# Halves side by side in the linear attention of a graph layer, with a new order of steps

## The reference

```python
x2 = _layer_norm(x, ln1_g, ln1_b)
q = (x2 @ wq + bq).reshape(B, L, N_HEAD, D_HEAD)
k = (x2 @ wk + bk).reshape(B, L, N_HEAD, D_HEAD)
v = (x2 @ wv + bv).reshape(B, L, N_HEAD, D_HEAD)
qp = _fourier_kernel(q, proj_mat)     # p = q @ proj_mat / 8, then cos(p), sin(p)
kp = _fourier_kernel(k, proj_mat)
kv = jnp.einsum('blhm,blhd->bhmd', kp, v)
attn = jnp.einsum('blhm,bhmd->blhd', qp, kv)
attn = attn.reshape(B, L, D_MODEL) @ wo + bo
```

## Time and profile before

| | before |
|---|---|
| median of 3 runs | 1335.42 us (1334.34 to 1340.76) |
| profiled execution, its time | 1334.61 us |
| its span | 1332.8 us |
| mean granted TensorE clock | 0.971 |
| PE busy | 94% of the span |
| DVE, ACT, POOL busy | 57%, 47%, 26% |

### The profile page before, as it was taken

The page is one execution under the profiler, slowest core; times in us unless marked ns, Lnnn a source line. Parts: engine busy times, 40 slices in busy tenths (PEclk is TensorE's granted clock), DMA queues, the critical chain, the costliest instruction groups (busy, mean ns, idle before and its releaser), DMA issues. The chain is left out here.

```text
span 1332.8 us, 19542 instructions
## 1 busy us (share of the span) xinstructions
PE 1247.7 (94%) x7017; PEld 1088.1 (82%) x7017; DVE 766.2 (57%) x1212; ACT 631.6 (47%) x917; POOL 340.5 (26%) x296
## 2 busy tenths in 40 slices
PE   6989889999999999999957999799999999899997
PEld 4556689999999999999946787699997887788874
DVE  7979625455655556565553376577774321556546
ACT  8175534555555555555554533332233442455544
POOL 1400003241423232332220201056662433021000
PEclk9999999999999999999976999899999799999999
DMA  8011310111020202020214645432335232620112
GB/s 207 10 29 25 78 36 1 33 35 54 12 66 0 66 0 66 0 66 0 67 45 150 216 151 172 137 107 81 92 91 192 74 93 62 211 72 14 50 32 93
DMA packets 72193, 99.41 MB, mean 75 GB/s; under 512 B 27241, under 2 KB 52165, under 8 KB 71631
## 3 DMA queue, kind: packets, MB, share of 16 engines
q1 hardware_dynamic: 68684, 86.11, 22.5%
q0 software_dynamic: 3456, 12.58, 3.1%
HBM read 77.04 MB, written 21.63 MB: 74 GB/s over the span
## 5 line engine op out<-in xcount | busy, mean ns | idle before, releaser
L1140 POOL TENSOR_TENSOR cos_sin_lo<-cos_sin,cos_sin_hi 125x1024 fp32r<-125x1024 f32 (+1 forms) x40 | 95.8, 2396 | 351.2 <-ACT cos_sin_hi L1214 351.2
L1201 ACT ACTIVATE cos_sin<-part_turn 125x512 f32<-125x512 f32 (+1 forms) x80 | 50.1, 627 | 152.7 <-DVE part_turn L1329 152.7
L468 PE MATMUL p_cnt<-hot_s,hot_d 125*125 125x418 bf16 x540 | 113.8, 361 | 1.8 <-DVE hot_d L401 1.8
L705 PE MATMUL p_h<-x 128*125 128x512 f32 x400 | 109.3, 400 | 0.0
L399 DVE TENSOR_SCALAR hot_s<-iota_h,ends 125x1250 bf16<-125x1250 f16 x180 | 98.2, 546 | 14.6 <-PE p_cnt L468 12.5
L468 PEld LDWEIGHTS p_cnt<-hot_s,hot_d 125*125 125x125 bf16 x540 | 63.3, 140 | 51.6 <-DVE hot_d L401 40.6
L1414 PE MATMUL p_w<-x,mix_hi_v 128*128 128x416 f32 (+1 forms) x384 | 105.2, 355 | 0.0
L1414 PE MATMUL p_w<-x,mix_hi_k 128*128 128x416 f32 (+1 forms) x384 | 104.2, 352 | 0.0
L1414 PE MATMUL p_w<-x,mix_hi_q 128*128 128x416 f32 (+1 forms) x384 | 104.1, 352 | 0.0
L966 PE MATMUL rows_in_psum<-h_hi,a_lo 125*125 125x342 f32 x300 | 96.8, 323 | 3.0 <-DVE a_lo L910 3.0
L1327 DVE TENSOR_SCALAR whole_turns<-p_p 125x512 f32<-125x512 f32 (+1 forms) x80 | 54.4, 680 | 77.0 <-PE p_p L1465 74.4
(11 more groups left out here) (302 smaller groups left out, 3169.8 us busy)
## 6 DMA issues: line engine op xcount, KB each, us to landing
x_in<-in_x_dram SPq DMA_DIRECT2D x30, 448.0 KB
attn_dram<-attn_t SPq DMA_DIRECT2D x8, 625.0 KB, 3.9
at_in<-attn_dram SPq DMA_DIRECT2D x10, 500.0 KB, 4.6
x_rows<-in_x_dram SPq DMA_DIRECT2D x10, 448.0 KB
x_in<-gnn_dram SPq DMA_DIRECT2D x10, 448.0 KB
out_dram<-rows SPq DMA_DIRECT2D x10, 448.0 KB
mix_in_v<-in_L_mix_wv_dram SPq DMA_DIRECT2D x8, 512.0 KB, 6.0
mix_in_k<-in_L_mix_wk_dram SPq DMA_DIRECT2D x8, 512.0 KB, 4.7
```

Of the source, the lines that this page charges most:

```text
L468: last = pe.matmul(p_cnt[0:T, t % 2, n, 0:w], hot_d[:, j, 0:T], hot_s[:, j, a:a + w], start=False, stop=False)
L705: last = pe.matmul(p_h[0:T, i % 2, n, :], left[i % 2][:, k, :], right[:, k, cols], start=(k == 0 and m == 0), stop=(k == K8 - 1 and m == 2))
L1140: pool.tensor_tensor(full(cs_lo, k), full(cs, k), f32(full(cs_hi, k)), ALU.subtract).then_inc(s_cslo[0], 1)
L1201: act.activation(step_view(cs, k, 1), rows(part, k), ACT.Sin, scale=TWO_PI)
```

## The change

Three products lose one of their three matmul terms. A high part and a low part now lie side by side in one operand, and the half of the array that held the other head or zeros holds the second part.

- `v_both` has, for each head, 64 columns of high part and 64 of low part. `accumulate_kv` multiplies them by the low and the high features of that head alone, 256 columns, into one of two banks of `p_kv_at`. The two halves of its output are added up later, in SBUF: ACT copies one half (`kv_sum`), DVE adds the other (`add_kv`), and both split the sum into `kv_both`.
- `kv_both` has high and low part side by side. `attend` takes the features' low and high part, 8 matmuls a step. The output of each head has two halves, in the two partition halves. ACT's `keep_attention` copies one, 64 partitions, for each head, and the new `add_attention` on DVE adds the other. `s_atk`, for which the next `attend` waits, is now given by DVE. `p_at` is the second bank of `p_kv_at`, so `accumulate_kv(j, 0)` waits for it too.
- `q_both` has a head's high part in one partition half and its low part in the other; `proj_both` has the projection in both. `query_phases` has 4 matmuls. ACT and DVE write the queries in halves of 64 partitions.
- All four compute engines get a new order in `pair`. `cos_sin` is cut in two, `sines` and `keep_hi`. `key_phases` of step k+2 stands at the start of round k, no longer at its end. On DVE `phases` comes one place sooner, and the splits of the graph weight (`low_of_w`, `high_of_w`) are spread over the last pass.

Each product now also holds the term lo*lo.

```diff
-        q_hi = sb("q_hi", [128, N], F32R)
-        q_lo = sb("q_lo", [128, N], F32R)
+
+        q_both = sb("q_both", [128, 2, N], F32R)
+        proj_both = sb("proj_both", [128, 2, KMAP], F32R)
         v_t = sb("v_t", [128, N])
-        v_hi = sb("v_hi", [T, NT, 128], F32R)
-        v_lo = sb("v_lo", [T, NT, 128], F32R)
+
+        v_both = sb("v_both", [T, NT, 2, 2, DH], F32R)
...
+        kv_sum = sb("kv_sum", [128, 4, DH])
+
+        kv_both = sb("kv_both", [128, 4, 2, DH], F32R)
...
-        p_kv = ps("p_kv", [128, 512])
-        p_at = ps("p_at", [128, 512])
+        p_kv = ps("p_kv_at", [128, 2, 512])
+        p_at = p_kv[:, 1]
```

ACT and GpSimd:

```diff
+            pool.wait_ge(s_prep, 3)
+            for n, half in enumerate((proj_lo, proj_hi)):
+                pool.tensor_tensor(proj_both[:, n], f32(half[:, 0]), f32(half[:, 1]), ALU.add).then_inc(s_prep, 1)
...
-                keep_lo(j, 0)
...
+                if more:
+                    keep_lo(j + 1, 0)
...
+            keep_lo(0, 0)
...
                 act.wait_ge(s_tr, 4 * j + 4)
+                act.activation(kv_sum[:], p_tr[:, :, DH:2 * DH], ACT.Copy, scale=1.0 / KMAP).then_inc(s_kvs, 1)
+                act.wait_ge(s_kvs, 2 * j + 2)
                 for h in range(2):
-                    last = act.activation(kv_hi[:, 2 * h:2 * h + 2, h * DH:(h + 1) * DH],
-                                          p_tr[:, 2 * h:2 * h + 2, h * DH:(h + 1) * DH], ACT.Copy, scale=1.0 / KMAP)
+                    last = act.activation(kv_both[:, 2 * h:2 * h + 2, h], kv_sum[:, 2 * h:2 * h + 2], ACT.Copy)
                 last.then_inc(s_trhi, 1)
...
-            def cos_sin(j, k):
+            def sines(j, k):
...
+
+            def keep_hi(j, k):
                 act.wait_ge(s_cs, done(j, k))
...
-                act.activation(attn_t[:, c * CHUNK:(c + 1) * CHUNK], p_at[:, 0:CHUNK], ACT.Copy).then_inc(s_atk, 1)
+                for h in range(2):
+                    head = slice(h * DH, (h + 1) * DH)
+                    last = act.activation(attn_t[head, c * CHUNK:(c + 1) * CHUNK], p_at[head, h * CHUNK:(h + 1) * CHUNK], ACT.Copy)
+                last.then_inc(s_atc, 1)
```

The queue of ACT at the end of a pass:

```diff
                 keep_attention(j, 2)
-                cos_sin(j, 9)
                 if more:
+                    sines(j + 1, 0)
                     keep_v(j + 1, 2)
-                else:
-                    gnn_w_high(5)
+                    keep_hi(j + 1, 0)
+                high_of_w(5)
                 keep_attention(j, 3)
                 if more:
-                    cos_sin(j + 1, 0)
+                    sines(j + 1, 1)
                     keep_run(KEY, j + 1, 2)
-                else:
-                    gnn_w_high(6)
+                high_of_w(6)
                 keep_attention(j, 4)
-                if more:
```

DVE, the new and the changed operations, and the middle of its queue:

```diff
-                hi, lo, s = (k_hi, k_lo, s_klo) if which == KEY else (q_hi, q_lo, s_qlo)
-                dve.scalar_tensor_tensor(lo[:, a:a + w], p_w[:, n, 0:w], bias[which][:, bass.ds(j, 1)], f32(hi[:, a:a + w]),
-                                         ALU.add, ALU.subtract).then_inc(s, 1)
+                if which == QUERY:
+                    for h in range(2):
+                        head, other = slice(h * DH, (h + 1) * DH), slice((1 - h) * DH, (2 - h) * DH)
+                        last = dve.scalar_tensor_tensor(q_both[other, h, a:a + w], p_w[head, n, 0:w], bias[which][head, bass.ds(j, 1)],
+                                                        f32(q_both[head, h, a:a + w]), ALU.add, ALU.subtract)
+                    last.then_inc(s_qlo, 1)
+                else:
+                    dve.scalar_tensor_tensor(k_lo[:, a:a + w], p_w[:, n, 0:w], bias[which][:, bass.ds(j, 1)], f32(k_hi[:, a:a + w]),
+                                             ALU.add, ALU.subtract).then_inc(s_klo, 1)
...
+            def add_kv(j):
+                dve.wait_ge(s_kvs, 2 * j + 1)
+                dve.scalar_tensor_tensor(kv_sum[:], p_tr[:, :, 0:DH], 1.0 / KMAP, kv_sum[:], ALU.mult, ALU.add).then_inc(s_kvs, 1)
 
             def keep_kv(j):
                 dve.wait_ge(s_trhi, 4 * j + 4)
                 for h in range(2):
-                    block_h = (slice(None), slice(2 * h, 2 * h + 2), slice(h * DH, (h + 1) * DH))
-                    last = dve.scalar_tensor_tensor(kv_lo[block_h], p_tr[block_h], 1.0 / KMAP, f32(kv_hi[block_h]),
-                                                    ALU.mult, ALU.subtract)
+                    last = dve.tensor_tensor(kv_both[:, 2 * h:2 * h + 2, 1 - h], kv_sum[:, 2 * h:2 * h + 2],
+                                             f32(kv_both[:, 2 * h:2 * h + 2, h]), ALU.subtract)
                 last.then_inc(s_trlo, 1)
+
+            def add_attention(j, c):
+
+                dve.wait_ge(s_atc, STEPS * j + c + 1)
+                for h in range(2):
+                    head, other = slice(h * DH, (h + 1) * DH), slice((1 - h) * DH, (2 - h) * DH)
+                    here = attn_t[head, c * CHUNK:(c + 1) * CHUNK]
+                    last = dve.tensor_tensor(here, here, p_at[other, h * CHUNK:(h + 1) * CHUNK], ALU.add)
+                last.then_inc(s_atk, 1)
...
+                keep_lo(j, 5)
+                low_of_w(1)
                 copy_kv(j)
-                keep_lo(j, 5)
+                phases(j, 7)
+                add_kv(j)
                 keep_kv(j)
-                phases(j, 7)
+                low_of_w(2)
```

PE:

```diff
-                    for m, (left, right) in enumerate(((proj_lo, q_hi), (proj_hi, q_lo), (proj_hi, q_hi))):
-                        last = pe.matmul(p_p[:, k % 2, h * CHUNK:(h + 1) * CHUNK], left[:, h, :], right[:, c * CHUNK:(c + 1) * CHUNK],
-                                         start=(m == 0), stop=(m == 2))
+                    for m in range(2):
+                        last = pe.matmul(p_p[:, k % 2, h * CHUNK:(h + 1) * CHUNK], proj_both[:, m], q_both[:, h, c * CHUNK:(c + 1) * CHUNK],
+                                         start=(m == 0), stop=(m == 1))
...
                 if k == 0:
                     pe.wait_ge(s_kvt, j)
+                    pe.wait_ge(s_atk, STEPS * j)
                 pe.wait_ge(s_trlo, 4 * j + (1, 2, 2, 3, 3)[k])
                 pe.wait_ge(s_cslo[k % 2], lo_done(j, k))
                 hi, lo = keys_view(cs_hi, k % 2), keys_view(cs_lo, k % 2)
                 for i in range(2):
-                    for m, (left, right) in enumerate(((v_lo, hi), (v_hi, lo), (v_hi, hi))):
-                        last = pe.matmul(p_kv[:], left[:, 2 * k + i, :], right[:, i].rearrange("p h c m -> p (h c m)"),
-                                         start=(k == 0 and i == 0 and m == 0), stop=(k == STEPS - 1 and i == 1 and m == 2))
+                    for m, right in enumerate((lo, hi)):
+                        for h in range(2):
+                            last = pe.matmul(p_kv[:, h, 0:2 * KMAP], v_both[:, 2 * k + i, h].rearrange("p a d -> p (a d)"),
+                                             right[:, i, h].rearrange("p c m -> p (c m)"),
+                                             start=(k == 0 and i == 0 and m == 0), stop=(k == STEPS - 1 and i == 1 and m == 1))
                 last.then_inc(s_added, 1)
...
                 for b in range(4):
-                    cols = slice(b * CHUNK, (b + 1) * CHUNK)
-                    for m, (left, right) in enumerate(((kv_lo, cs_hi), (kv_hi, cs_lo), (kv_hi, cs_hi))):
-                        last = pe.matmul(p_at[:, 0:CHUNK], left[:, b, :], right[:, k % 2, cols],
-                                         start=(b == 0 and m == 0), stop=(b == 3 and m == 2))
+                    h = b // 2
+                    for m, right in enumerate((cs_lo, cs_hi)):
+                        last = pe.matmul(p_at[:, h * CHUNK:(h + 1) * CHUNK], kv_both[:, b].rearrange("p a d -> p (a d)"),
+                                         right[:, k % 2, b * CHUNK:(b + 1) * CHUNK],
+                                         start=(b % 2 == 0 and m == 0), stop=(b % 2 == 1 and m == 1))
                 last.then_inc(s_at, 1)
...
                 half = K8 // 2
-                for k in range(3):
-                    query_run(j, k)
-                    accumulate_kv(j, k)
+                for k in range(STEPS):
                     if k + 2 < STEPS:
                         key_phases(j, k + 2)
-                for k in range(3, STEPS):
-                    if more:
+                    else:
+                        query_phases(j, k + 2)
+                    if k < 3:
+                        query_run(j, k)
+                    elif more:
                         value_run(j + 1, k - 3)
                     accumulate_kv(j, k)
-                    query_phases(j, k + 2)
+                query_phases(j, 7)
                 if more:
-                    value_run(j + 1, 2, 0, half)
+                    value_run(j + 1, 2, 0, 2)
                 transpose_kv(j)
                 if more:
-                    value_run(j + 1, 2, half, K8)
+                    value_run(j + 1, 2, 2, K8)
                 attend(j, 5)
```

(84 more changed lines are left out.)

78 lines of the change are left out of this document (37 added, 41 removed).

## The result

| | before | after |
|---|---|---|
| median of 4 runs of each | 1334.88 us (1333.56 to 1340.76) | 1314.05 us (1311.03 to 1319.77) |
| profiled execution / its span | 1334.61 / 1332.8 us | 1319.77 / 1318.0 us |
| PE, DVE, ACT busy | 94%, 57%, 47% | 92%, 65%, 50% |

The ratio is 0.984, 95% interval 0.981 to 0.988: faster by 1.6%. The prediction was 1310 us, range 1286 to 1324. The total is 4 us from the forecast, but three terms of the forecast's sum were 4.5 to 6 us off each, and their errors cancelled in part. That it came so close is partly luck.

What follows compares the result with a forecast made beforehand. TensorE was taken to bound the kernel, a steady pass being the sum of its matmuls. Seven passes 26 us less, clock 6 more, last pass 6 less: 1335.4 - 26 gives about 1310 us, range 1286 to 1324.

Steps and rivals of the forecast that it cites:

- the signs that it named: Expected trace marks: `kv_t` copies 60 to 61 us apart, matmuls 0.12 apart, waits ahead of `attend`, last pass 55 to 60.
- Which engine bounds, and the matmul terms: Steady pass: TensorE bounds; fewer matmuls in three products save 5.7 us, leaving 58.1 us of matmul time.
- The two waits: End of a pass: TensorE waits for DVE's additions queued behind `phases`, about 0.35 and 1.9 us.
- The kv chain and the transposes' wait: Before `attend(5)`: the 0.52 us wait at the transposes goes; the longer kv chain costs 0.1 us, bounds 0 and 1.
- A steady pass: Loop pass over a head pair: 58.1 + 2.4 + 0.1 = 60.6 us, 3.75 less; seven passes give 26 us less.
- The clock, +6: Half of seven 1.9 us waits lower TensorE's granted clock, 1.7 us each: 6 us more, bounds 0 and 12.
- The last pass, -6: Last pass, written apart: its ACT, DVE and GpSimd chain ends some 6 us sooner, bounds 0 and 8.
- The first pass: TensorE's 1.78 us wait ahead of `accumulate_kv(0)` only moves: `key_phases(2)` waits about 1.5 us for `phases(0)`.
- Rival 1: End-of-pass waits stay hidden, the third `phases` operation getting through before GpSimd: 49 us less, 1286 us; chance 0.2 with neighbourhood.
- Rival 4: `accumulate_kv`: 256-column matmuls cost as much as 512-column ones, 36 us more, 1346 us; chance 0.05 together with Rival 3.
- Rival 3: End-of-pass waits lower the clock and it stays low, from about 9.5 us longer 1342 us up; 0.05 with Rival 4.

Runs made afterwards that it cites:

- g1: Changed kernel, DVE's attention additions ahead of `phases`, ACT's `keep_attention(3)` ahead of `keep_hi`, SyncE's attention store behind the next key weights' load: 1300.9 us.
- f3: Changed kernel with one more DVE operation in `phases(j+1,1)`, to lengthen TensorE's wait ahead of `attend(9)`: 1334.65 us.
- f2: Changed kernel with the first two graph weight splits moved behind `keep_kv` in the last pass, on ACT and DVE: 1313.2 us.
- f4: Changed kernel with the halves of values and key sums alone taken back, `accumulate_kv` and `attend` in three terms: 1315.2 us.
- e2: Changed kernel with the low part of cos/sin of the next pair's step 0 made by DVE instead of GpSimd: 1306.7 us.
- e3: Changed kernel with the queries' halves alone taken back, three matmuls a head and step: 1324.0 us.
- g2: g1 with the last pass reordered on ACT and DVE: `kv_t` copied behind `phases(5)`, additions ahead of `phases`, weight splits later: 1295.1 us.

## Why the prediction was right, point by point

The total was right, with luck in it: the 6 us for the clock did not come and made up for 5.9 us that the steady passes did not give. The way there was right for the matmuls, for which engine bounds and for where TensorE waits. Of the signs that it named, the waits and the 0.12 us between starts were there; the `kv_t` copies stand 61.44 us apart (60 to 61 forecast), the last pass takes 62.6 us (55 to 60 forecast), and the clock did not fall in a steady pass.

- **Which engine bounds, and the matmul terms: right.** Groups of 160 and 320 matmuls stand 0.12 us apart, and a 256-column one costs no more than in the earlier trace rows. Check from g1: 59.10 less its one wait (0.62 + 0.16) is 58.3, predicted 58.1. From before, 64.35 less 0.68, that is 5.4 us a pass, predicted 5.7.
- **The two waits: right in place and cause, too small.** Predicted 0.35 + 1.9 and 0.15 of loss; read 0.59 + 2.13, and some 0.16 us of restart each, 3.0 against 2.4. I had priced a pair of additions at 0.72 to 0.75 us and it took 0.84, twice in the chain. The Trainium skill, page "VectorE: DVE Perf Modes", section "Two Vector instructions with no wait between them", was cited for this with no row behind it. The rows agree now: each half starts in another quadrant than the one ahead, two halves take 0.84 together, 0.41 each end to end, where the earlier trace rows had two operations overlap.
- **The kv chain and the transposes' wait: right.** No PE wait is left there in a steady pass.
- **A steady pass: 61.44, predicted 60.6.** 2.91 us less a pass instead of 3.75, over seven passes 5.9 us less gained. The mis-sized terms are the waits and some 0.2 us of matmul time.
- **The clock, +6: wrong in this kernel.** I took the term from a single event, the 1.78 us of the earlier trace rows. In the trace of after the granted clock is 1.00 in all steady passes although each has a wait of 2.13 us. The bound of 0 held. That a wait 0.6 us longer is followed by a fall in all seven passes of f3's trace shows how near the term was to the other end; the bound of 12 us was too low, since seven falls cost 7 x 2.8 = 20 there. Two falls were in no term: in the trace of after the clock was at 0.50 for 6 us of the first pass, and from 655 us to the end of the stage, where before it still had a mean of 0.82 from 645 to 710. The Trainium skill, page "TensorE: Matmul & The Clock Gate", Part 1, has the gate follow "how busy the PE has been recently"; the traces agree in kind, and none tells here which wait of 1.3 to 2.1 us is followed by a fall.
- **The last pass, -6: mis-sized.** From the end of the last loop pass to the end of the stage it fell from 64.1 to 62.6 us, by 1.5. I had named both causes (`copy_kv` behind `low_of_w(1)`, an addition ahead of each `attend`) and priced them too low: the first is 4.8 us (f2), the second part of the 4.6 us of tail that comes with the halves (f4 to after). The low clock of that tail is likely another part, and I had no term for it.
- **The first pass: right.** From the first transposes to the end of the seventh pass the gain is 20.1 us, of which six steady passes of 2.91 give 17.5, so the first gave 2.7. The 1.78 us of waiting went, and the wait for `phases(0)` in its place is 0.23 us in after and 1.32 in f2, where the clock did not fall.
- **The rivals.** Rival 1's mechanism could be made: without the collision e2 takes 1306.7. Rival 4 fell with the pitches. Rival 3 did not happen; in f3, with 0.6 us more of waiting, its falls came and used up the whole gain (median 1334.65 us), though none lasted the 7.5 us longer that it asked for.

Sum of the errors: +5.9 (passes), -6 (clock), +4.5 (last pass) = +4.4 us against 26 promised, and the stretch from the first transposes to the end of the stage shows 21.7.

What stays open: what sets off the clock's fall behind one wait and not behind another of the same length, even in the same code, and how the 4.6 us of tail divide between additions, queue places and the clock.

## What to carry to other kernels

Taking matmuls out of a bound TensorE pays only as far as the halves' extra steps stay off an in-order queue that it waits for: here one set of halves paid in full, and the other paid 0.94 of some 4 us a pass until its additions and copies were moved ahead of work that nobody waits for (with g1's order a pass is 3.3 us shorter than f4's). After each wait removed, look for the next chain around the whole loop, the transfers' queue too: it was 1 us behind. And keep TensorE's waits short where you can: those of 2.73 us were followed by a fall of the granted clock more often than those of 2.13, and a wait of 2.73 us cost 2.8 us more than itself where it fell.

## What the runs showed of the hardware

- With a wait of 2.73 us instead of 2.13 in front, the granted clock was 0.50 for some 6.2 us in each of seven passes of f3's trace; with 2.13 us it stayed at 1.00 in all of seven in one kernel (after) and fell in two of seven in another (e3). Behind waits of 1.70 and 1.26 us in the same code it fell to 0.50 in one trace (after, 193 to 199 us) and stayed at 1.00 in another (f2).
- At 0.50 the 250-column matmuls of `attend` started 0.21 us apart, at 1.00 0.12.
- A VectorE operation with two SBUF inputs that meets GpSimd took 1.92 instead of 0.69 us (512 elements) and 3.33 instead of 1.22 (1024), and GpSimd's own rose in the second case, from 2.33 to 3.15 us: it had started 0.24 us into another VectorE operation with two SBUF inputs (649.55, 1.20 us, in g2).
- Two 64x250 additions with a PSUM input, in alternating partition halves, took 0.84 us together.
